# VectorE's routing work for a batch, spread over more slots of the order

## What is computed

```python
x = _layernorm(x + attention(x))            # per batch, 8 tiles of 128 tokens
logits = x @ w_router                       # 32 experts
top1 = argmax(logits); gate = softmax(logits)[top1]
pos = cumsum(one_hot(top1))[top1] - 1       # place of the token in its expert's list
accepted = pos < C                          # C = 320
slot = where(accepted, top1 * C + pos, E * C)
buf[slot] = x                               # rows sent to their expert
out = x + where(accepted, gate * expert(buf)[slot], 0)
return _layernorm(out)
```

## Time and profile before

| what | value |
|---|---|
| median of 3 runs | 2505.95 us (2505.47 to 2508.99) |
| the profiled execution's own time | 2510.11 us |
| its span in the trace | 2508.0 us |
| busy: PE, DVE, ACT, POOL | 94%, 64%, 40%, 67% |
| PE's waits for DVE's maxima of L1117 and L1121 (largest rows) | 18.5, 13.8, 13.4 us |
| DVE's 64 normalisations, L1199 | 395 / 424 / 2455 ns (min / median / max) |

### The profile page before, as it was taken

How to read it: one execution, slowest core, us unless ns; L and a number is a source line. 1 busy time by engine, 2 the same in 40 slices (tenths; PEclk the granted TensorE clock), 3 DMA queues, 4 the chain that set the end, 5 groups by cost and what they waited for, 6 DMA issues and landing times.

```text
span 2508.0 us, 36804 instructions
## 1 busy us (share of the span) xinstructions
PE 2345.6 (94%) x11528; PEld 1517.6 (61%) x11528; DVE 1602.7 (64%) x4618; ACT 1015.1 (40%) x1992; POOL 1678.9 (67%) x1623
## 2 busy tenths in 40 slices
PE   6999999999999999999999999999999999949996
PEld 4555575556655665566555665566556655537774
DVE  4677657765676667765776567666776577335553
ACT  3445424443444334542444334433444344212222
POOL 1688756975787757875797568766787579623444
PEclk8999999999999999999999999999999999969998
DMA  3222100200011001100020001100110001224652
GB/s 87 60 64 81 39 14 14 73 18 14 18 49 37 18 10 39 47 18 13 18 69 18 14 18 51 35 18 9 43 43 18 18 14 55 68 79 155 193 180 68
DMA packets 96818, 118.96 MB, mean 47 GB/s; under 512 B 12289, under 2 KB 75783, under 8 KB 96625
## 3 DMA queue, kind: packets, MB, share of 16 engines
q1 hardware_dynamic: 89712, 99.98, 14.5%
q0 software_dynamic: 6912, 16.64, 1.9%
HBM read 46.91 MB, written 37.90 MB: 34 GB/s over the span
## 4 chain that ended last, share of the span: by engine, by line
PE 76%; DVE 13%; issue 6%; POOL 1%; ACT 1%; DMA 0%; DVEq 0%; SPq 0%; POOLq 0%; ACTq 0%
PE value_ps L722 18%; PE misc_ps L744 9%; PE turned_ps L699 9%; PE turned_ps L702 8%; PE misc_ps L621 8%; PE turned_ps L891 6%; PE row_ps L674 6%; PE turned_ps L674 3%; PE misc_ps L734 3%; DVE masked_row L1117 2%; DVE q_hl L1098 2%; DVE q_hl L1097 2%; DVE rinv L1151 1%; PE misc_ps L770 1%; DVE x L1199 1%
## 5 line engine op out<-in xcount | busy, mean ns | idle before, releaser
L964 ACT ACTIVATE probs<-turned_ps 128x512 f32<-128x512 f32 (+2 forms) x1280 | 652.1, 554 | 815.2 <-PE turned_ps L702 801.2
L504 POOL TENSOR_TENSOR half_sums<-half_sums,probs 128x1024 f32<-128x1024 f32 (+3 forms) x512 | 832.4, 1626 | 33.2 <-ACT probs L964 15.9
L722 PE MATMUL value_ps<-probs,lat_keys 128*64 128x512 f32 (+3 forms) x3072 | 597.7, 511 | 0.0
L699 PE MATMUL turned_ps<-q_hl,lat_hi 128*128 128x512 f32 (+2 forms) x1280 | 529.7, 414 | 1.5 <-ACT fold_v L1009 1.5
L702 PE MATMUL turned_ps<-q_max,lat_lo 65*128 65x512 f32 (+2 forms) x1280 | 483.7, 378 | 2.5 <-DMA q_max<-both_rows 2.5
L479 POOL TENSOR_SCALAR_AFFINE_SELECT probs<-probs 128x256 f32<-128x256 f32 x512 | 210.3, 411 | 405.0 <-ACT probs L964 404.1
L1117 DVE CUSTOM_DVE_ANT_0 masked_row<-row_ps,future 128x512 bf16<-128x512 f32 (+4 forms) x707 | 347.3, 511 | 189.6 <-PE row_ps L674 184.2
L499 POOL TENSOR_TENSOR half_sums<-probs 128x768 f32<-128x768 f32 (+1 forms) x128 | 269.4, 2105 | 140.8 <-ACT probs L964 118.2
L674 PE MATMUL row_ps<-lat_hi,q_hl 128*128 128x512 f32 (+4 forms) x1026 | 324.3, 356 | 33.0 <-DVE neg_max L1117 18.5
L722 PEld LDWEIGHTS value_ps<-probs,lat_keys 128*64 128x64 f32 x3072 | 190.5, 139 | 265.3 <-issue 199.8
L699 PEld LDWEIGHTS turned_ps<-q_hl,lat_hi 128*128 128x128 f32 x1280 | 244.6, 191 | 137.3 <-issue 107.9
(11 more groups left out here) (191 smaller groups left out, 2652.3 us busy)
## 6 DMA issues: line engine op xcount, KB each, us to landing
q_max<-q_hl SPq DMA_DIRECT2D x256, 128.0 KB
slots_x<-router SPq DMA_DIRECT2D x8, 1290.0 KB, 6.0
ex_x<-slots_x SPq DMA_DIRECT2D x64, 129.0 KB, 2.4
x_in<-in_L_attn_x_bld SPq DMA_DIRECT2D x8, 1024.0 KB, 5.5
layer_out<-x_in SPq DMA_DIRECT2D x8, 1024.0 KB, 4.5
ex_w<-in_L_ffn_w_gate SPq DMA_DIRECT2D x32, 256.0 KB, 3.7
ex_w<-in_L_ffn_w_up SPq DMA_DIRECT2D x32, 256.0 KB, 3.8
ex_w<-in_L_ffn_w_down SPq DMA_DIRECT2D x32, 256.0 KB, 4.3
```

The lines of the kernel that those rows point to most:

```text
L504: nc.gpsimd.tensor_tensor(total, total, now[:, :, q0:BANK], ALU.add).then_inc(added, 1)
L699: nc.tensor.matmul(scores_of(n, h), lat_hi[b % 2][:, keys], q_hl[gp % 2][:, heads, cols], start=True, stop=False)
L722: mm = nc.tensor.matmul(value_ps[h * LD:(h + 1) * LD, q0:BANK], lat_keys[b % 2][:, j, :], probs[:, n % NPROBS, h, q0:BANK], start=(j == 0) ...
L964: nc.scalar.activation(probs[:, n % NPROBS, heads, q0:BANK], scores_of(n, h), ACT.Exp).then_inc(exp_done, 1)
```

## The change

The eight normalisations of a batch get a slot each: `NORMALISE_AT` puts tiles 0 and 1 into slots 10 and 11 of pair 1, tiles 2 and 3 into slots 0 and 1 of pair 2, tiles 4 to 7 into its slots 4 to 7. Each tests `rstd_ready` by itself, and the last of a half sets `x1_ready`. `destinations` is cut in two: `addresses` (two of the address steps, gate and token number) in slot 10 of pair 3, the rest in slot 11. The third group of turned tiles (the second half's first) moves from slot 7 of pair 2 to slot 9. In the last batch the order is nearly the same: there only the gate and the token number come before the last address step.

```diff
+    NORMALISE_AT = [(1, 10), (1, 11), (2, 0), (2, 1), (2, 4), (2, 5), (2, 6), (2, 7)]
...
-                for use, t in zip([(hf, kd) for hf in range(2) for kd in range(KD)], (3, 5, 7, 10)):
+                for use, t in zip([(hf, kd) for hf in range(2) for kd in range(KD)],
+                                  (3, 5, 9, 10)):
                     late[t].append(("x1T", b - 1, *use))
...
-            def normalise(b, hf):
-                dve.wait_ge(rstd_ready, b * 2 + hf + 1)
-                for i in range(hf * HPB, (hf + 1) * HPB):
+            def normalise(b, tiles):
+                for i in tiles:
+                    dve.wait_ge(rstd_ready, b * 2 + i // HPB + 1)
                     last = nc.vector.tensor_scalar(x1[:, i, 0:D], x1[:, i, 0:D], mean_var[:, i, 0:1], rstd[:, i:i + 1],
                                                    ALU.subtract, ALU.mult)
-                last.then_inc(x1_ready, 1)
+                    if i % HPB == HPB - 1:
+                        last.then_inc(x1_ready, 1)
...
-            def destinations(b):
+            def addresses(b):
 
                 settle()
                 step(nc.vector.scalar_tensor_tensor(rt[:, 5, :], rt[:, 3, :], float(C), rt[:, 4, :], ALU.mult, ALU.add))
                 step(nc.vector.tensor_scalar(rt[:, 7, :], rt[:, 4, :], float(C), FAR, ALU.is_ge, ALU.mult))
+                nc.vector.tensor_scalar(x1[:, :, GATE], rt[:, 2, :], 0.5, None, ALU.mult)
+                step(nc.vector.tensor_copy(x1[:, :, TOKEN].bitcast(I32), token_f[:, :]))
+
+            def destinations(b):
+
                 settle()
                 step(nc.vector.scalar_tensor_tensor(rt[:, 8, :], rt[:, 5, :], float(SLOTS), rt[:, 7, :], ALU.add, ALU.add))
-                nc.vector.tensor_scalar(x1[:, :, GATE], rt[:, 2, :], 0.5, None, ALU.mult)
-                step(nc.vector.tensor_copy(x1[:, :, TOKEN].bitcast(I32), token_f[:, :]))
                 settle()
...
+                    if b and (p, t) == (3, 10):
+                        addresses(b - 1)
...
-                    if b and (p, t) in ((1, 10), (2, 4)):
-                        normalise(b - 1, p - 1)
+                    if b and (p, t) in NORMALISE_AT:
+                        normalise(b - 1, [NORMALISE_AT.index((p, t))])
```

More of the change, by code:

```diff
@@ L404, in load_weights @@
                 for m, w in enumerate((w_gate, w_up, w_down)):
-                    sp.dma_start(ex_w[k][:, m], w[e].rearrange("(k p) f -> p k f", p=P)).then_inc(ex_loaded[k], 16)
+                    sp.dma_start(ex_w[k][:, m], w[e].rearrange("(k p) f -> p k f", p=P)
+                                 ).then_inc(ex_loaded[k], 16)
             def load_rows(e):
@@ L1317, in _ @@
                     count_tiles(LAST)
+                    addresses(LAST)
                     destinations(LAST)
@@ L1321, in _ @@
                 if use[0] == "rest" and use[2] == NT - 1:
-                    normalise(LAST, 0)
+                    normalise(LAST, range(HPB))
                     variance(LAST, 1)
-                    normalise(LAST, 1)
+                    normalise(LAST, range(HPB, NT))
             def copy_rows(e):
```

## The result

The change made the kernel slower: 2529.34 us (median of 7 runs, 2518.01 to 2534.64) against 2507.24 (7 runs, 2505.47 to 2512.0) before, a ratio of 1.0082 with a 95% interval of 1.0065 to 1.01. The forecast was 2527.0. The profiled execution of after took 2529.34 (its span is 2527.3), 19.2 us more than the 2510.11 of before's.

The account below looks back on a forecast made before the run. TensorE, busy 94% of the span, was taken as the bound, so its waits and half-speed time count. 7 x (2.3 for pair 2 + 0.7 for pair 3) = 21 us gave 2527; range 2511 to 2537, with the clock 2510 to 2546.

Parts of the forecast that it names:

- the wait of slot 9: Pair 2: PE's moved transposes wait 2.46 a batch for DVE's subtraction of q's high half, after slot 9's two maxima.
- Rival C: Slot 9's bank is free earlier and PE's 1.97 goes without a successor: 12 us faster, 2494; chance 0.12.
- The tiles: Pair 2: tiles 4, 6 short, 5, 7 long; PE's 1.97 in slot 6 becomes 1 to 2 in slot 8.
- the long one: The 2.46 us normalisation in the earlier trace, lying inside POOL's addition of 387.43; tile 5 was taken to wait like it.
- rival A: Tile 6 loses to POOL's product (1.3 a batch) and slot 9's wait brings a clock fall (1.35): 2544; chance 0.20.
- The addresses: Pair 3, slot 10: a new 2.1 wait at the next pair's slot 0, the 1.40 goes: net +0.7 a batch.
- the case in which L1253 is ahead of POOL: Pair 3: L1253 takes 0.17, the new wait is 0.95 and pair 3 gains 0.45 a batch.
- my one row: Earlier trace, pair 3: L1253 started at 710.41, POOL's product at 710.43, yet L1253 took 1.31; taken as POOL going first.
- No net change, within 10: PE's clock over the whole kernel: half-speed falls shift but cancel, widening the range by about 10 either way.
- A's fall behind the wait: Pair 2: PE's wait of 2.5 in slot 9 brings a short clock fall, 1.35 a batch; part of a 0.20 rival.
- B's gain: Pair 2's logits keep full clock in all six batches that lose it now: 16 us less, 2511; chance 0.08.
- a long wait shortly before the logits is no help: Pair 2: the prediction's argument against the logits keeping full clock, a rival of 16 us less and chance 0.08.

Follow-up runs that it names:

- e1: The kernel before with only the third group of turned tiles moved from slot 7 to slot 9 of pair 2: 2530.65 us.
- e3: The changed kernel with q of pair 2 moved from slot 8 to slot 7: 2507.15 us.
- e4: The changed kernel with tile 5 normalised right behind tile 4 in slot 4 of pair 2: 2520.62 us.
- e2: The kernel before with only the destinations cut in two and the addresses in slot 10 of pair 3: 2529.41 us.
- e8: e3 with all address steps back in slot 11 of pair 3, as before the change: 2507.09 us.
- e6: e2 with the eight transposes of the keys in pair 7 made three times over: 2525.69 us.

## Why the prediction was right

The time, 2527.0 forecast and 2529.34 measured, came for its largest part, the wait of slot 9, out of the mechanism that was named. That the terms of pair 3 and of the clock fit as well is in part luck.

*The slot-9 wait.* Taken as 2.46, measured 2.38 in all seven batches. Even its composition held: from slot 9's first maximum at 400.33 to the end of the subtraction at 402.79 there are 2.46, as in the earlier trace rows. e1 shows that it is the moved transposes alone, e3 that it is q's place ahead of them. Rival C, in which the bank comes free early, fell: DVE stands 0.93 idle before slot 9, and the maxima and the subtraction still are the whole wait.

*The tiles.* Tile 4 took 0.41 (taken as unhindered; it met only the last 0.26 of a POOL addition), tile 5 2.38 (taken: as long as the long one), tile 6 0.37 (0.32 of DVE's time taken), tile 7 0.68 (0.8 taken). The wait moved from slot 6 to slot 8 and fell from 1.97 to 1.61; the 1.61 is in the forecast "1 to 2". e4 confirms that tile 5's meeting with POOL is behind it. The part of rival A that stood on DVE did not come: tile 6 was 0.23 ahead of the product and went first.

*Pair 2 and pair 3.* Pair 2 was to cost 2.3 a batch, 16.1 in all, and cost 13.4: PE stands still 14.2 longer, worth 16 by the line above, and the clock, at half for 37.5 us instead of 47.8, gave some 4 back. Pair 3 was to cost 0.7, 4.9 in all, and cost 4.6, but not in the way that was forecast (below). Together 18.0 against the sum's 21; the start-up's 1.7, no part of the change, brings the profiled span closer to it.

*The addresses.* In every batch a wait of 2.1 was to come, because L1253 in its new place loses to POOL, and one of 1.40 was to go. This step failed. The 1.40 was there in batches 2 and 3 alone, and the new wait is 1.94 in batches 6 and 7 and 0.59 to 0.79 in the other five, near the 0.95 that the prediction gave for the case in which L1253 is ahead of POOL. The clock doesn't part the two kinds: batch 5 kept 1.00 in all of pair 3 (1516.18:1546.58), with a wait of 0.79. What parts them is which of the small instructions meets POOL. In batch 2 the selection of 716.91 let L1255 of 716.90 go in 0.16, and the addition of 717.29 let the cast, L1257, of 717.26 go in 0.16. In batch 6 L1255 started as close, 1804.46 against 1804.47, and took 0.44; L1256 (L1253 of before), at 1804.81, then got ahead of the addition of 1804.84 in 0.16, and the cast behind it waited 1.25 for that addition. The other batches of each kind show the same durations. So the seven new waits are 7.6 together instead of 14.7, and the old ones that went are 2.8 instead of 9.8: PE stands still 5.5 longer in pair 3, against the 4.9 of the sum. That they agree is luck. On who goes first, the rule of the Trainium skill (SBUF — State Buffer, "Who interferes with whom") that the prediction set aside did better than my one row: 716.90 against 716.91, 717.26 against 717.29 and 1804.81 against 1804.84 were won by DVE. But 1804.46 against 1804.47 and the race of the earlier trace rows (710.41 against 710.43) were lost. Races of 0.01 to 0.03 are not to be read from these starts.

*The clock.* "No net change, within 10" held for the kernel as a whole: 64.8 us of half clock after 71.7, worth 2.6. But it held because two effects that I gave to opposite rivals came together. A's fall behind the wait came: in four of after's seven batches, and in all seven of e1, the clock falls within 1.7 us of the end of slot 9's wait, which the value products at 404.38 show. B's gain came in those very batches: the logits, which took 4.62 in batch 1 of before (with the fall in them), take 3.76. My argument that a long wait shortly before the logits is no help did not hold; where the fall came with the wait, the logits kept full speed. In the other three batches they kept it too, and the fall came 0.3 to 1.0 us behind them. In before it had come inside them in five batches, and not only after them, as the prediction has it.

As a step for single edits "no net change" is wrong. e2 lost 17 us by it, in e8 it moved from one pair to the next, and the parts do not add: the turned tiles cost 23 alone, the addresses 22 alone, and both with the tiles 22. Had the change been e2's, I would have forecast 2512 by the same working and been out by 17 with a range of 10 either way.

What stays open: why the same pair loses its clock in one schedule and keeps it in another. The runs show that the falls shift with work added far away (e6) and with waits removed in the next pair (e8), and what they cost; no run here says beforehand where they will come. The spread of the tiles was not run by itself; its worth is seen only as after against e1 (3 us less of pair 2) and in e4.

## What to carry to other kernels

When a user of a shared buffer moves, price it by what it now stands behind: follow that buffer's last reader through its engine's queue, as q's subtraction behind two maxima here, and ask whether the earlier user can move too (one slot won back 22 us). Spreading an engine's work out is worth something only where the pieces come clear of the other engine that blocks them; one piece that begins just behind a long POOL instruction cost nearly as much (1.61) as four together (1.97). And where differences of less than 1% are read, put the time at half clock beside the waits before calling either the cause, and judge single parts of a change by both.

## What the hardware showed that was not expected

- The clock's share was of the size of the waits': by the line above 27 us of pairs 2 and 3 of before against 35 for standing still, and 44 against 38 in e2. Between those two kernels the seven stretches of pair 2, with the same waits of 16.0 us, differ by 8.8 us, with 47.8 and 68.3 us at half clock. Adding 6 us of matrix work elsewhere to e2 did not make it slower (2525.69 against 2529.41).
- Right behind a wait of 2.38 us the clock was granted at 0.50 for 404.50 to 407.90, and eight value products took 3.63 instead of 1.94. The same wait in batch 4 of after was not followed so: there the fall came 9.5 us later.
- VectorE's small instructions beside POOL turn on starts that differ by 0.01 us: the same order of instructions cost PE 0.79 us in one batch and 1.94 in another.
- A normalisation takes 0.37 to 2.38 us in its plain form and 0.44 to 0.48 in the form that also writes a sum, beside the same POOL work.
